# Decoder layer on one core: scores and transposed scores of the attention steps issued in pairs, exponentials in pairs

## The reference

```python
def reference(x, ctx_4096, ...):
    # self attention
    qkv = x @ attn_qkvw + attn_qkvb            # q, k, v per head
    scores = einsum('bhqd,bhkd->bhqk', q, k) / sqrt(32)
    probs = softmax(scores, axis=-1)
    ctx = einsum('bhqk,bhkd->bhqd', probs, v)
    x = layernorm(x + ctx @ attn_ow + attn_ob)
    # product of the two fake-quantised operands, [512 x 1024] @ [1024 x 1024] per sequence
    x = layernorm(x + fake_quant(x) @ fake_quant(ctx_4096))
    # base matrix, and 2 of 8 low-rank experts of rank 16 picked by a router
    x = layernorm(x + x @ W_base.T + b_base + experts(x))
```

## Time and profile before

| | |
|---|---|
| median of 3 runs | 731.79 us (731.21 to 733.44) |
| profiled execution, own time | 733.02 us |
| its span | 731.2 us |
| mean granted TensorE clock | 0.996 of full speed |
| TensorE busy | 97% |
| VectorE busy | 64% |
| ScalarE busy | 58% |
| GpSimd busy | 33% |

### The profile page before, as it was taken

The page is one execution under the profiler, slowest core; times in us unless marked ns, Lnnn a source line. Parts: engine busy times, 40 slices in busy tenths (PEclk is TensorE's granted clock), DMA queues, the critical chain, the costliest instruction groups (busy, mean ns, idle before and its releaser), DMA issues.

```text
span 731.2 us, 11765 instructions
## 1 busy us (share of the span) xinstructions
PE 710.5 (97%) x3512; PEld 530.4 (73%) x3512; DVE 464.9 (64%) x831; ACT 426.5 (58%) x919; POOL 243.6 (33%) x189
## 2 busy tenths in 40 slices
PE   6999999999999999999999999999999988999996
PEld 5778668668677677686686686767676766888884
DVE  6877557456476575584574575476877776665564
ACT  4458668677686686685686776764554763211111
POOL 5370150060061052042042077554735543111111
PEclk9999999999999999999999999999999999999999
DMA  8746435436426436336334277719442513122101
GB/s 291 219 132 219 118 82 198 117 82 201 123 69 203 107 88 193 91 108 190 92 108 123 72 250 222 239 44 323 152 143 87 179 54 116 59 96 77 57 30 57
DMA packets 55732, 98.97 MB, mean 135 GB/s; under 512 B 10896, under 2 KB 21392, under 8 KB 54800
## 3 DMA queue, kind: packets, MB, share of 16 engines
q1 hardware_dynamic: 55408, 98.13, 43.8%
q10 hardware_dynamic: 288, 0.39, 0.2%
HBM read 56.41 MB, written 16.65 MB: 100 GB/s over the span
## 4 chain that ended last, share of the span: by engine, by line
PE 73%; issue 13%; DMA 3%; DVE 3%; POOL 3%; SPq 3%; ACT 1%; ACTq 0%; POOLq 0%; DVEq 0%
PE bank L468 43%; PE bank L594 8%; PE bank L564 8%; PE bank L608 8%; PE bank L719 2%; POOL xb L1176 2%; SPq L252 1%; PE bank L520 1%; DMA wb_raw<-in_wbT 1%; DMA kp<-k_lo 1%; DMA big_raw<-in_xT 1%; PE bank L693 1%; SPq L226 1%; DVE st L1428 1%; POOL mv L1157 0%
## 5 line engine op out<-in xcount | busy, mean ns | idle before, releaser
L1354 DVE TENSOR_REDUCE m_col<-bank 128x1 f32<-128x512 f32 x256 | 173.2, 688 | 81.3 <-PE bank L564 80.4
L859 ACT ACTIVATE probs<-bank 128x512 f32<-128x512 f32 x256 | 152.1, 596 | 121.2 <-PE bank L594 118.5
L864 ACT ACTIVATE bank<-bank,m_col 128x512 f32<-128x512 f32 x256 | 169.3, 661 | 17.2 <-DVE m_col L1354 16.3
L468 PE MATMUL bank<-big_hi,w_hi 128*128 128x512 f32 x384 | 156.6, 408 | 6.3 <-DVE big_lo L1251 5.5
L468 PE MATMUL bank<-big_lo,w_hi 128*128 128x512 f32 x384 | 152.5, 397 | 0.0
L468 PE MATMUL bank<-big_hi,w_lo 128*128 128x512 f32 x384 | 151.0, 393 | 0.0
L564 PE MATMUL bank<-kp,qp 96*128 96x512 f32 x256 | 101.5, 397 | 2.1 <-DMA kp<-k_lo 1.5
L594 PE MATMUL bank<-qp,kp 98*128 98x512 f32 x256 | 101.0, 398 | 0.0
L1116 POOL TENSOR_SCALAR c_raw<-c_raw,sc 128x1024 f32<-128x1024 f32 x16 | 19.2, 1201 | 230.4 <-DMA c_raw<-in_ctx 226.3
L468 PEld LDWEIGHTS bank<-big_hi,w_hi 128*128 128x128 f32 x384 | 73.3, 191 | 25.2 <-DVE big_lo L1251 5.5
L468 PEld LDWEIGHTS bank<-big_hi,w_lo 128*128 128x128 f32 x384 | 72.8, 190 | 17.0
(11 more groups left out here) (137 smaller groups left out, 1056.2 us busy)
## 6 DMA issues: line engine op xcount, KB each, us to landing
w_raw<-in_wqkv SPq DMA_DIRECT2D x7, 1536.0 KB, 8.4
c_raw<-in_ctx SPq DMA_DIRECT2D x16, 512.0 KB, 4.2
qp<-q_hi SPq DMA_DIRECT2D x128, 64.0 KB, 2.0
kp<-k_hi SPq DMA_DIRECT2D x124, 64.0 KB, 2.0
big_raw<-in_xT SPq DMA_DIRECT2D x16, 256.0 KB, 6.3
qp<-q_lo SPq DMA_DIRECT2D x64, 64.0 KB, 2.0
c_scratch<-c_q SPq DMA_DIRECT2D x16, 256.0 KB, 2.2
r_all<-r_scratch SPq DMA_DIRECT2D x64, 64.0 KB, 2.0
```

The costliest lines, as they stand in the source:

```text
L468: mm = nc.tensor.matmul(dst, lhs[a], rhs[b], start=(k == 0 and n == 0) if first is None else False, stop=(k == last_k and n == 2))
L859: nc.scalar.activation(probs[:, j, t, :], bank(ST0 + i % 2), ACT.Exp).then_inc(sem["exp_ok"], 1)
L864: nc.scalar.activation(bank(max_bank(s, n)), bank(max_bank(s, n)), ACT.Exp, bias=m_col[:, n:n + 1], accum_out=l_col[:, 1 - par, n:n + 1]). ...
L1354: nc.vector.reduce_max(m_col[:, n:n + 1], bank(max_bank(s, n)), AX, negate=True).then_inc(sem["rowmax"], 1)
```

## The change

The two slot functions give the same q for scores n and n+1 of an even n, and the same q to both kinds of scores. The two `if`s that place one score per q become `while`s, so that all that have this q are issued. At such a place TensorE now issues score n, score n+1, transposed score n, transposed score n+1. There are eight such places in a steady step, at q = 2, 7, 12, 18, 23, 29, 34 and 40. ScalarE's loop gets `while`s as well, so its order becomes E(n), E(n+1), ES(n), ES(n+1). Step 1 keeps its score slots, step 2 its transposed slots; steps 16 and 17 keep everything.

```diff
         def score_slot(n, second):
-            return 6 + (34 * n + 14) // 15 if second else 2 + (38 * n + 14) // 15
+            return 6 + (34 * n + 14) // 15 if second else 2 + 38 * (n // 2) // 7
         def transposed_slot(n, third):
-            return 8 + (39 * n + 14) // 15 if third else 2 + 3 * n
+            return 8 + (39 * n + 14) // 15 if third else 2 + 38 * (n // 2) // 7
...
-                    if maxima and done < NS and q == score_slot(done, second):
+                    while maxima and done < NS and q == score_slot(done, second):
                         score(done)
                         done += 1
...
-                    if finish and turned < NS and q == transposed_slot(turned, third):
+                    while finish and turned < NS and q == transposed_slot(turned, third):
                         score_t(turned)
                         turned += 1
...
-                    if finish and turned < NS and q == transposed_slot(turned, third) + 1:
+                    while finish and turned < NS and q == (transposed_slot(turned, third) + 1 if proj else 3 * turned + 3):
                         exp_scores(turned)
                         turned += 1
-                    if maxima and done < NS and q == (score_slot(done, isinstance(s, int) and s == 1) + 3 if proj else 3 * done + 3):
+                    while maxima and done < NS and q == (score_slot(done, isinstance(s, int) and s == 1) + 3 if proj else 3 * done + 3):
                         exp_sum(done)
                         done += 1
```

## The result

| | before | after |
|---|---|---|
| median of 5 runs in turn, us | 731.8 (731.21 to 733.44) | 736.07 (735.46 to 738.08) |
| ratio, 95% interval | 1 | 1.0062 (1.0050 to 1.0074) |
| profiled execution, its span, us | 733.02, 731.2 | 735.8, 734.0 |
| steps 3 to 15 by the contexts, us | 371.79 | 374.66 |

The account below looks back on a forecast made before the run. TensorE was taken as the bound; from a median of 731.79 us, merging saves 2.9 and waits add 5.3, net 2.4: 734.2 us, 734.3 with the clips. Range 730.8 to 737.2, the forecast's own part 733.0 to 735.6.

Parts of the forecast that it names:

- The bound: Steady steps 3 to 15: TensorE, busy 97% of the span, bounds the kernel; a step is as long as its matmuls.
- The merging, 0.22 us a step: TensorE, steady steps: 11 projection groups move behind another group, each saving 0.02 us; 2.9 us over 13 steps.
- rival 3: Switching between kinds of matmuls costs nothing, the wait comes as forecast: 737.1 us, slower; chance 0.10.
- The wait, 0.15 and 0.26: TensorE waits for ScalarE at scores 3 and 9, behind gaps of two groups: 0.41 us a step, 5.3 over 13.
- Rival 1: The wait is half as dear, only the matmul being held: 0.21 us a step, 731.7 us, no change; chance 0.20.
- rival 2: The wait doesn't come, as paired E leaves ScalarE earlier; only merging counts: 728.9 us, faster; chance 0.08.
- rival 4: The second E of a pair starts only when the first ended, 0.60 instead of 0.49 us: 737.2 us; chance 0.10.
- The steady steps together: Steps 3 to 15: 2.9 us saved by merging and 5.3 us added by the waits.
- Step 2, taken as 0 with 0.1 us to either side: Step 2 pairs only its scores: two or three merged runs, no score on the edge; 0 us, 0.1 either side.
- The long clip, at most 0.03 us in a step: VectorE's longest clip, 2.25 us, delays maximum 9, ES(9) and E(10), using up three groups' 0.42 us: at most 0.03.
- The halves of q and k, nothing: Taken behind maximum 5 and 11 as before, waiting for the same projection groups; packing transfers start as before: no cost.
- The sum: Whole kernel: profiled 733.02 - 2.9 + 5.3 = 735.4 us; as a median 734.2, with the clips 734.3.

Follow-up runs that it names:

- e7_interleave_waits: e2_interleave with VectorE's packing-transfer waits ahead of its projection wait, the clip behind maximum 9 instead of 8, and step 2's old score slots; 729.19 us.
- e10_step2_pairs: e7_interleave_waits with the scores of step 2 paired again as in the changed kernel; 730.07 us.
- e11: e9_gaps_of_three with the clip behind maximum 9 instead of 8 and VectorE's packing-transfer waits ahead of its projection wait; 728.53 us.
- e9_gaps_of_three: e3_step2 with the eight places at q = 0, 6, ..., 42, three projection groups between any two, and the maxima's transpose behind the last group; 729.27 us.
- e5_dose_waits: e4_dose with VectorE's four packing-transfer waits moved ahead of its wait for the projection; 744.24 us.
- e3_step2: The changed kernel with the scores of step 2 back at their old slots; 735.15 us.
- e1_alternate: The changed kernel with ScalarE taking E(n), ES(n), E(n+1), ES(n+1) in steps 3 to 15; 732.71 us.
- e4_dose: e3_step2 with places at q = 2, 7, 12, 16, 20, 28, 32, 36: five gaps of two groups instead of two; 752.87 us.
- e2_interleave: The changed kernel with each place issuing score n, transposed score n, score n+1, transposed score n+1 in steps 3 to 15; 731.83 us.
- e8_before_waits: The kernel before with only VectorE's packing-transfer waits moved ahead of its wait for the projection; 732.24 us.

## Why the prediction was right, step by step

**The bound.** Right. TensorE stayed the bound: the steady steps grew by the waits that were put before it.

**The merging, 0.22 us a step.** Right. The groups take 0.70, 0.68, 0.68, and the pitch between two scores or two transposed scores is 0.23, as taken (0.63 - 0.40 for a row of two). The three versions without a wait in a steady step (e7, e10, e11) take 28.37 to 28.41 us against 28.60: 0.19 to 0.23. Before, the contexts of steps 4 to 13 also wait for E(15), which after doesn't have. That is no rival for this gain: steps 3, 14 and 15 lack the wait and take 28.60 as well. So rival 3, in which the switch costs nothing, is refuted. The Trainium skill ("TensorE: Matmul & The Clock Gate", "Back-to-back issue gap") has an isolated spacing that depends on the columns alone; the trace disagrees, as 0.70 against 0.68 for three matmuls of 512 columns shows.

**The wait, 0.15 and 0.26.** Right, in place, number and size: at score 3 and 9, 26 waits, 0.15 and 0.25 lost by the timeline. In total 28.82 - 28.38 = 0.44 us a step, against 0.41; 0.02 of it is the wait in step 5. The idle time of the weight loads at score 3 is 0.20, below the 0.3 to 0.5 that I said would show. Rival 1 (half of it) and rival 2 (none) fall by this, rival 4 by E to E 0.49. The time alone would have said otherwise: 736.07 is nearer to the 737.1 and 737.2 of rivals 3 and 4 than to 734.3. The steps, 28.82 instead of their 29.0, decide for the forecast. That the gaps of two are the cause isn't only read: e9_gaps_of_three takes them away and the waits go but for one behind a long clip, e5_dose_waits has five of them and pays in proportion.

**The steady steps together.** Forecast +2.4 us (5.3 - 2.9), measured 374.66 - 371.79 = 2.9. Of the difference of 0.5 us, 0.25 is the wait in step 5 and the rest 0.02 us in each step.

**Step 2, taken as 0 with 0.1 us to either side.** Wrong in size: some 0.9 us by the medians (after against e3_step2, e10_step2_pairs against e7_interleave_waits), 0.75 by the context. I counted merged runs and found no score on the edge, because I took ScalarE's chain of a steady step. In step 2 the maximum comes late, behind the clip and the conversion of the context, which GpSimd stretches. Before, score 3 lay two groups and the transposes of v further on, and that was its room.

**The long clip, at most 0.03 us in a step.** Wrong in size. Step 5 of after shows all links (VectorE, then ScalarE, then the weight load of score 13):

```profile
149.35 2.47 DVE L1326 TENSOR_SCALAR c_raw<-c_raw 128x1024 f32<-128x1024 f32 x1
151.74 1.87 DVE L1354 TENSOR_REDUCE m_col<-bank 128x1 f32<-128x512 f32 x3
```

```profile
152.45 0.66 ACT L864 ACTIVATE bank<-bank,m_col 128x512 f32<-128x512 f32 x1 [1.23 <-DVE m_col L1354]
```

```profile
154.93 0.19 PEld L564 LDWEIGHTS bank<-kp,qp 96*128 96x128 f32 x1 [0.41 <-ACT bank L864]
```

The chain is the one that I described, but I took 2.25 us, the longest clip of one execution, for the longest there is. Here it is 2.47, in e3_step2 2.92. My 0.42 us of room were used up at 2.25, so each further tenth is paid: 0.25 us in this step, 0.7 in e3_step2's. In e9_gaps_of_three 0.7 is lost at 2.68 already, so the room isn't the same in every version.

**The halves of q and k, nothing.** True of after, but by luck: for a reason that I did not have. The maxima behind them come 0.44 to 0.55 us later than they need, and only E(7) ahead of ES(6) covers that. e1_alternate takes the cover off and ends 1.9 us above its expectation; e4_dose loses 8.6. Nor do the packing transfers always leave room: in e3_step2 one held up step 15.

**The sum.** By medians the change costs 4.3 us. The steady steps' 2.9 and step 2's 0.9 make 3.8; for the other 0.5 I have no row. The interval of the ratio, 1.0050 to 1.0074, is 3.7 to 5.4 us, so 3.8 isn't ruled out. The two profiled executions are only 2.8 apart; that of before was 1.2 above its median and that of after 0.3 below. So the forecast, 1.8 us too low, had its mechanism and its main terms, and missed step 2 and part of the scatter of the clips. Its range held the result only because it was drawn up to rivals 3 and 4, which were false.

## What to carry to other kernels

When work is gathered into fewer places, the count of places is the gain and the smallest gap between two of them is the price: write the chain from one place to the next link by link, and compare it with each gap, in every kind of step and not only in the steady one. A chain with tenths of a microsecond to spare needs the longest case of each link over several executions, not of one. And an engine's waits that are met early belong ahead of the wait that comes last; whether they are met early in every step has to be looked up.

## What the runs showed of the hardware

**A clip that lasts as long as its neighbour.** The same clip on VectorE, 128x1024 in place, takes 0.68 or 0.69 us where GpSimd has no work beside it and up to 2.9 where it has. In step 5 of after, GpSimd and VectorE, and for comparison VectorE in step 4:

```profile
148.87 2.40 POOL L1069 TENSOR_TENSOR w_lo<-w_raw,w_hi 128x1024 fp32r<-128x1024 f32 x1
```

```profile
120.52 0.68 DVE L1326 TENSOR_SCALAR c_raw<-c_raw 128x1024 f32<-128x1024 f32 x1
```

GpSimd's operation ends at 151.27, the clip at 151.82, 0.55 behind. In e3_step2 the two ends are 150.95 and 151.51, 0.56 apart; in before 378.55 and 379.10. The 13 traces hold 208 such clips. 105 have nothing on GpSimd beside them: 0.68 or 0.69 us. 102 begin while a GpSimd instruction runs, and end 0.54 to 0.62 us behind its end, whatever their length. One (e2_interleave, at 434.73) begins 0.03 us ahead of GpSimd's instruction, and takes 0.68. So a clip that comes second does nearly all its work once the other is done: it does not run at half speed beside it. The Trainium skill ("SBUF — State Buffer", "Who interferes with whom") has the ports that these two engines share as an exclusive lock, where VectorE's instruction uses both of its port pairs: the later one stands still. The traces agree. No run here moved GpSimd's operation on purpose; what stands for a test is that the overlap differs from step to step and from execution to execution.

**Four satisfied waits cost 0.44 to 0.55 us on VectorE**, by division 0.11 to 0.14 each, where they stand behind the wait that is met last (e4_dose against e5_dose_waits). Ahead of it they cost nothing that shows where VectorE is early. Where VectorE arrives late, their order changes nothing: e8_before_waits begins the halves as late as before.
